# A routed expert kernel on one core: GpSimd's scatters into the expert lists, one or two at a time between weight splits instead of four in a row

## The reference, cut to what matters

```python
x1 = cond_adapter(x)                     # 256 -> 64 -> 256 per sequence, plus x
h  = rmsnorm(x1); q, k, v = h @ qkv_w    # 16 heads, 4 kv heads, 64 wide, rope, window, sink
x2 = x1 + attn(q, k, v) @ proj_w
h2 = rmsnorm(x2)
topv, topi = top_k(h2 @ gate_w + gate_b, 4)      # 4 of 32 experts for each token
gw = softmax(topv)
y2 = sum over experts e of gw[:, e] * ((silu(h2 @ Wg[e]) * (h2 @ Wu[e])) @ Wd[e])
out = x + x2 + y2
```

## Time and profile before

| | |
|---|---|
| median of three runs | 1194.93 us (1192.10 to 1195.15) |
| the profiled execution, its own time | 1196.22 us |
| its span in the profile | 1194.3 us |
| PE busy | 990.4 us (83%) |
| DVE busy | 766.7 us (64%) |
| POOL busy | 716.1 us (60%), of these scatters L660 125.3 us, splits L667 121.1 us |
| ACT busy | 455.6 us (38%) |
| part one, until the last scatter into the lists is issued | to 632.2 us |
| the experts | 660 to 1162 us |

### The profile page before, as it was taken

One profiled execution on the slowest core, in us unless ns is written; L12 is line 12 of the kernel. 1 busy time (PEld: TensorE's weight loads), 2 busy tenths in 40 slices (PEclk: granted clock), 3 DMA queues, 4 the chain that ended last, 5 costly groups with the idle time before them and its releaser, 6 DMA issues.

```text
span 1194.3 us, 18647 instructions
## 1 busy us (share of the span) xinstructions
PE 990.4 (83%) x6190; PEld 798.9 (67%) x6190; DVE 766.7 (64%) x1712; ACT 455.6 (38%) x1128; POOL 716.1 (60%) x676
## 2 busy tenths in 40 slices
PE   3789799998999999998833878888978888988985
PEld 2557576776777676776622767777767777877774
DVE  3868487786867777784661555656656556556577
ACT  1133243434243353424511444444435344444441
POOL 3426346858586776767584656666666666666650
PEclk9779899999999999998965999998999999998998
DMA  5328877565657666556566756465655556552399
GB/s 175 86 65 275 311 256 202 186 185 191 190 171 240 205 199 198 188 170 215 196 211 230 240 186 243 155 237 183 230 194 195 189 186 215 187 189 74 86 349 337
DMA packets 110951, 239.46 MB, mean 200 GB/s; under 512 B 19311, under 2 KB 48388, under 8 KB 110119
## 3 DMA queue, kind: packets, MB, share of 16 engines
q1 hardware_dynamic: 84042, 192.03, 49.1%
q0 software_dynamic: 19760, 40.32, 10.9%
q10 hardware_dynamic: 7056, 5.91, 1.6%
HBM read 140.66 MB, written 90.32 MB: 193 GB/s over the span
## 4 chain that ended last, share of the span: by engine, by line
PE 57%; DVE 19%; issue 8%; POOL 4%; DMA 4%; another core or an unknown queue 4%; ACT 3%; SPq 0%; POOLq 0%; DVEq 0%; ACTq 0%
PE gbank L858 9%; PE gbank L990 8%; PE scores L990 6%; PE gbank L1009 4%; DVE ring L1349 4%; PE gbank L783 4%; PE scores L819 4%; PE scores L1009 3%; POOL lists L660 3%; PE gbank L999 2%; PE gbank L761 2%; DVE in_part L1580 2%; DVE mid L1588 2%; PE scores L999 1%
## 5 line engine op out<-in xcount | busy, mean ns | idle before, releaser
L705 POOL DMA_INDIRECT pick_rows<-rows_out,pair_row x158 | 163.5, 1035 | 141.3 <-ACT rows_out L1218 98.6
L698 POOL DMA_INDIRECT rows_in<-x_rows,token_row x158 | 154.1, 975 | 54.5 <-issue 43.6
L667 POOL TENSOR_TENSOR ring<-ring 128x512 fp32r<-128x512 f32 x96 | 121.1, 1280 | 72.5 <-ACT ring L1159 71.1
L660 POOL DMA_INDIRECT lists<-entry,slot_i x128 | 125.3, 979 | 38.8 <-issue 34.2
L858 PE MATMUL gbank<-w_o,ring 128*128 128x256 f32 x512 | 128.1, 407 | 14.8 <-DVE ring L1332 12.1
L990 PE MATMUL gbank<-ring,in_part 128*128 x480 | 139.4, 428 | 0.0
L990 PE MATMUL scores<-ring,in_part 128*128 x486 | 138.0, 421 | 0.0
L783 PE MATMUL gbank<-h_t,w_qk 128*128 128x512 f32 x480 | 120.8, 405 | 7.3 <-DVE h_t L1336 4.2
L858 PEld LDWEIGHTS gbank<-w_o,ring 128*128 128x128 f32 x512 | 103.2, 205 | 35.2 <-ACT ring L1129 16.3
L1349 DVE SCALAR_TENSOR_TENSOR ring<-gbank,b_qk,rope 128x512 f32<-128x512 f32 x160 | 108.5, 743 | 5.3 <-PE gbank L783 5.1
L783 PEld LDWEIGHTS gbank<-h_t,w_qk 128*128 128x128 f32 x480 | 89.7, 192 | 29.9 <-issue 5.8
(11 more groups left out here) (189 smaller groups left out, 1917.8 us busy)
## 6 DMA issues: line engine op xcount, KB each, us to landing
w_parts<-ring SPq DMA_DIRECT2D x192, 256.0 KB
ring<-w_parts SPq DMA_DIRECT2D x32, 1536.0 KB
ring<-in_W_up SPq DMA_DIRECT2D x64, 256.0 KB
picks<-pick_rows SPq DMA_DIRECT2D x8, 2048.0 KB, 27.8
lists<-in_fill_slots SPq DMA_DIRECT2D x36, 256.0 KB, 4.9
ring<-in_W_down SPq DMA_DIRECT2D x32, 256.0 KB
q_r<-rot SPq DMA_DIRECT2D x16, 512.0 KB, 6.1
q_r<-ring SPq DMA_DIRECT2D x16, 512.0 KB
```

The costliest lines, as they stand in the source:

```text
L660: e.indirect_dma_start(out=lists, out_offset=bass.IndirectOffsetOnAxis(ap=slot_i[pb][:, k:k + 1], axis=0), in_=entry[pb][:, k, :], in_offs ...
L667: e.tensor_tensor(lower, lower.bitcast(F32), upper.bitcast(F32), ALU.subtract).then_inc(s_lower, 1)
L698: e.indirect_dma_start(out=rows_in[i % NG][:, :], out_offset=None, in_=x2_rows, in_offset=bass.IndirectOffsetOnAxis(ap=begun[:, i, 3:4].bi ...
L705: e.indirect_dma_start(out=pick_rows, out_offset=bass.IndirectOffsetOnAxis(ap=begun_row[:, i:i + 1] if i < AHEAD else pair_row[:, i:i + 1] ...
```

## The change

POOL's step `route_put` (four scatters, for one tile) becomes `put` (one scatter), and in the period and in the end of POOL's order the scatters stand one, two or three at a time between the splits. The scatters keep their order among themselves, and so do the splits and the pairs; the orders of the other four engines are untouched.

```diff
@@ ORDERS
     "POOL": ("""
         up pair pair pair pair pair up
     """, """
-        split split pair pair split split pair pair split split pair route_put split split split
-        route_put up route_put split split split route_put
+        split split pair pair split split pair pair split split pair put split put put split put put
+        split put put up put put put split put put split put put split put put
     """, """
-        split split split split split route_put split split route_put split route_put split split split
-        route_put split route_put route_put route_put route_put
+        split split split split split put put split put put split put put split put put split put put put split
+        put put put split put put split put put put split put put
     """),
@@
-         "route_list": GROUPS, "split": 3 * E, "load_third": 3 * E, "store_third": 3 * E}
+         "route_list": GROUPS, "put": NT * TOPK, "split": 3 * E, "load_third": 3 * E, "store_third": 3 * E}
-ROUTE = ("root", "route_turn", "route_pick", "route_count", "route_list", "route_put")
+ROUTE = ("root", "route_turn", "route_pick", "route_count", "route_list", "put")
@@ gpsimd_program
-        def route_put(t):
+        def put(n):
+            t, j = divmod(n, TOPK)
             r, s = ROOT_OF[t], t % TPM - ROOTS[ROOT_OF[t]][1]
-            pb = r % NPAY
+            pb, k = r % NPAY, s * TOPK + j
             w.wait_ge(s_slot_i, r + 1)
             w.wait_ge(s_fill, FILL)
-            for k in range(s * TOPK, (s + 1) * TOPK):
-                e.indirect_dma_start(
-                    out=lists, out_offset=bass.IndirectOffsetOnAxis(ap=slot_i[pb][:, k:k + 1], axis=0),
-                    in_=entry[pb][:, k, :], in_offset=None).then_inc(s_entry[pb], 16)
+            e.indirect_dma_start(
+                out=lists, out_offset=bass.IndirectOffsetOnAxis(ap=slot_i[pb][:, k:k + 1], axis=0),
+                in_=entry[pb][:, k, :], in_offset=None).then_inc(s_entry[pb], 16)
```

More of the change, by code:

```diff
@@ L106 @@
     """, """
-        split split pair pair split split pair pair split split pair route_put split split split
-        route_put up route_put split split split route_put
+        split split pair pair split split pair pair split split pair put split put put split put put
+        split put put up put put put split put put split put put split put put
     """, """
-        split split split split split route_put split split route_put split route_put split split split
-        route_put split route_put route_put route_put route_put
+        split split split split split put put split put put split put put put split put put put split
+        put put split put put split put put split put put
     """),
@@ L673, in gpsimd_program @@
                 pair(*k)
-            elif name == "route_put":
-                route_put(k)
+            elif name == "put":
+                put(k)
             elif name == "split":
```

## The result

| | before | after |
|---|---|---|
| median of ten runs | 1194.72 us (1191.51 to 1199.23) | 1185.58 us (1178.83 to 1189.57) |
| the profiled execution, its own time | 1196.22 us | 1188.5 us |
| its span | 1194.3 us | 1186.7 us |

The ratio after to before is 0.9921, 95% interval 0.9896 to 0.9945: faster by 0.8%, some 9 us, where no change was forecast.

A forecast was written before the change was run, and what follows sets the result against it. Bound: PE, ACT and DVE handovers in the middle periods, POOL's amount of work in the tail. Tail -0.2 and period 7 -0.1 gave -0.3 us, taking the median 1194.93 to 1194.6 us; range 1190.3 to 1199.2.

The forecast's parts named there:

- the price of the earlier up: Middle periods: up starts 2.4 us earlier on POOL, but the sums on PE start behind the scores anyway; priced at nothing.
- Its own sign of being wrong: Wrong if splits enter the middle periods' chain, the period changes over 0.5 us, or POOL waits for ScalarE in the tail.
- Period 7: Group 5's scatters, about 535 to 564 us: one fewer beside the moves; took 0.1 us gain, upper bound 1.77 us.
- the tail: POOL's last scatters and splits, 583.5 to 632.2 us: more blocks with single splits; net gain 0.2 us.
- splits 92 to 95: Tail: POOL reaches them at 596.8, 600.5, 605.4 and 609.2 us; waits for ScalarE priced 0, bound 1.5 us.
- scatter 111: Tail: group 6's last scatter moves behind split 95, making DVE's list of group 9 at most 0.7 us late; priced 0.
- The 4.12 us copy: DVE's copy of group 7's slots, 601.71 to 605.83 us: released 2.5 to 3.8 us earlier by single splits; priced 0.
- Split 71's delay: Middle periods: split 71 ends 1.2 us later, delaying its store and load 74; priced 0, upper end 1.5 us per period.
- C: Rival, six periods: split 71's delay reaches ScalarE's split and exponential through load 74; slower by 4 us or more, chance 0.10.
- the 4% of GpSimd: Chain of waits: GpSimd's share is 4%, said to be all L660, the scatters this change moves.
- B: Rival: fewer scatters beside moves and loads in period 7, PE keeps its upper clock; faster by 4 us, 1190.5, chance 0.15.

The follow-up runs named there:

- e2: Guarded kernel after (one register operation more per expert tile on PE) with up moved two scatters later; 0.9987 of the kernel before.
- e4: Guarded kernel after with the end of POOL's order as in the kernel before; 0.9923 of before, 1095.86 us, on the second chip.
- e5b: e5's program run again on the fourth chip, one with the hold (late releases behind long scatter runs); 1.0103 of before, 1208.41 us.
- e8: Guarded kernel before with ACT's two splits moved behind the softmax's exponential, POOL's order untouched; 0.9989 of before, 1204.81 us, third chip.
- e9: e8 plus, on POOL, one split set behind the third of the four scatters behind up; 0.9926 of before, 1195.18 us, third chip.
- c0: Kernel before with a guard on PE's wait for expert weights, one register operation more per expert tile; 1.0022 of before, 1197.78 us, first chip.
- c0b: The guarded kernel before, c0, run again on the third chip; 0.9993 of before.
- e1: Guarded kernel before with up moved ahead of the second four scatters, so eight run in a row; 1.0265 of before, 1227.04 us.
- e1b: e1 run again on the third chip; 1.0265 of before.
- e5: Guarded kernel after with one split moved per period, so five scatters run in a row behind up; 0.9917 of before, 1096.00 us, second chip.
- e6: Guarded kernel before with one split moved per period, breaking the run of four scatters behind up after three; 1.0009 of before, 1105.36 us, second chip.
- e7: Guarded kernel after with attend ahead of the sums on PE and ACT; 0.9826 of before, 1085.43 us, second chip.
- e8b: e8 run again on the fourth chip, one with the hold (late releases behind long scatter runs); 1.0020 of before.

## Why the prediction was wrong

Measured were 1185.58 us, under the whole range. **The step that failed** is the price of the earlier up: "Price nothing; the cover is the scores and what is ahead of them on PE, 2.4 us now." It followed up's output to one consumer, the sums on PE. That part holds: the sums follow the scores in both traces. It did not list what is queued behind the waiting squares on ACT: two splits, the copies and the softmax's exponential, and behind that DVE's softmax and apply. There was no cover there. Its own sign of being wrong came: from one project behind the sums to the next, periods 2 to 6, it is 66.5 to 69.0 us before and 65.8 to 67.4 after. e2 measured this way alone: up starts 8.0 us ahead of the sums (478.83 to 486.81) where it was 9.4 in after (473.50 to 482.91) and 7.9 in before (481.43 to 489.32), and 0.7 of the 0.8% are lost. The earlier trace rows had shown the symptom, a project of 5.38 us, and the chain's piece "sums" of 2.98 us where the matmuls take 1.98; I read it as work of PE. Period 4 of before was an experiment that lay open: there up began 9.1 us ahead of the sums and the run of four ended 1.2 us ahead of their end, so that neither wait was there; PE waited 1.39 us, and project took 3.69.

**The second cause** could not be priced from the text of the change, but its trace was there: the logarithm beginning 1.0 us behind a run of four in four of five periods, and in period 7, behind the run of eight from 545.26, this:

```profile
556.78 1.22 DVE L1364 TENSOR_REDUCE beside<-scores 128x16 f32<-128x1024 f32 x1 [4.40 <-remote]
...
556.84 1.08 ACT L1121 ACTIVATE ring<-gbank 128x512 f32<-128x512 f32 x2 [5.48 <-remote]
```

Both start 1.7 us behind the end of that run (555.12), with PE's scores of 549.31 long done. **Period 7** was priced at 0.1 with a bound of 1.77 from the moves. The lead grew by 1.26 there though its first project took 1.69 longer (5.41 against 3.72), so 2.95 us were won behind it. Breaking the run of eight fits that place and size, but it is argued: no experiment was made on period 7 alone. The wait for ScalarE was still 0.28 us: the moves' part of it was rightly small.

**Right:** the tail. It was priced at -0.2 us and came to -0.29 (10.84 less 10.55 of lead where it begins); POOL was busy 39.91 us in it against 39.71, with no wait for ScalarE. e4 agrees, 0.9923 without the new end. The end of POOL's order in the change above is not that of the kernel that ran, which is `sssss pp s pp s ppp s ppp s pp s pp s pp s` and 16 p. In the tail that makes blocks of 2, 2, 3, 3, 2, 2, 2 and 16: eight, as in the prediction, so its 0.2 us stand, but splits 92 to 95 are reached 1.4 to 2.7 us later, counted from the tail's start, than it says, with more cover for ScalarE, and scatter 111 stays ahead of split 95. The 4.12 us copy took 0.17, and nothing hung on it. Split 71's delay cost nothing, but the path that C names was in use: load 74 was issued 2.1 us later against the sums (492.38 to 482.91, before 496.73 to 489.32), ACT's split waited 3.00 us for it and kept the exponential behind it until 496.69, 1.7 us after its input was ready at 494.95. What covered it were DVE's two pairs, through at 500.2; POOL's next pair waited 0.54 us for DVE. L660 had 987 ns in the mean. One reading was off without a consequence: of the 4% of GpSimd in the chain of before, L660 holds 3%, not all.

**Half right:** up came earlier, but by 1.5 us against the sums and not 2.4. It now waits 1.08 us for its own input (L1288), so more scatters moved behind it would bring nothing.

**The rivals.** B, faster, had the sign and half of the mechanism: a project at the lower clock costs 1.66 us. It put the idle time at the moves, with one or two such projects, and gave 4.4 us. The packets of the scatters aren't what counts: e5b has the same scatters and loads as the kernel after and takes 1.8% longer (1208.41 to 1187.23) by one split's place. C did not occur.

## What to carry to other kernels

When an operation moves on one engine, follow its result into the queue of the engine that waits for it and price everything that stands behind the wait, not only the consumer that needs it. Where two waits end within 0.3 us of each other, removing one shows next to nothing (e2, 0.9987, has no hold; e8, 0.9989, has no late exponential) and only both together show the gain (e9, 0.9926): a null result does not clear a suspect. Do not let four or more of GpSimd's indirect DMAs run in a row where a handover that sets the pace falls, and repeat a small result on a second chip. Whether three in a row are harmless was not shown: in every trace here with a run of three near the sums, the run had ended 1.2 us or more before they did.

## What the runs showed of the hardware

- *Long runs of indirect DMAs on GpSimd hold back releases among other engines, on some chips.* The logarithm on ACT began 1.0 to 1.2 us behind the end of a run of four (before, c0, c0b, e8), 1.1 to 1.2 of five (e5b), 1.55 to 1.76 of eight (e1, e1b), up to 5.5 us after PE's sums had ended. On three chips it was seen, besides in the trace of before; on a fourth the runs of five in e5 held nothing. Not every release is held: in the kernel after, DVE's addition behind PE's project started at 541.37, at once, while the fifth scatter of a run of five ran. Nor does one split always end it: in e9 a run of seven ended at 543.67, a split and a single scatter followed until 546.11, and DVE began at 546.69 on scores that PE had finished at 542.85. What is held up was not found, nor whether the number of scatters counts or the moment at which the release falls into the run. The Trainium skill (Perfetto Trace Analysis, DMA Instruction — SWDGE (GPSIMD)) says that the recorded end of such a DMA is the end of its descriptors, not of the transfer; that leaves room for an after-effect, which no run here identifies.
- *The chip without the hold ran the kernel before in 1104.45 us*, against 1196 to 1205 us on the others. Part one was nearly the same there (its end at 635.14 in e6, 638.29 in c0); the 90 us are in part two, with its 316 indirect DMAs by GpSimd. The traces point at the same late releases: from 640 us on, ACT and DVE of c0 spent 141 us in 75 waits whose releaser the profile has no name for, those of before 152 us in 92, and in the four profiles of that chip (e4 to e7) there is not one; POOL waited 103 us for ACT's result rows in c0 and 10 us in e6. That the hold is the cause of the 90 us is still an inference, since no kernel was built to remove it in part two.
- *A stop of PE before project of 1.4 us never cost it clock in periods 2 to 6*: project took 3.69 to 3.72 us behind each. Of 31 stops of 1.8 to 2.5 us in seven profiles (before, c0, c0b, e2, e6, e8, e8b), 23 were followed by a project of 5.1 to 6.8 us and eight by one of 3.69. The length of the stop alone does not tell which.
